# Global attention in a four-block transformer kernel: the row maxima are turned by a transposing transfer instead of TensorE, two steps earlier, and the output copy moves between two exponentials

## The reference, cut to what matters

```python
q = rope((x @ Wq).reshape(b, s, 32, 8)) * 8 ** -0.5      # 32 half-heads of 8 features
k = rope((x @ Wk).reshape(b, s, 32, 8))
v = (x @ Wv).reshape(b, s, 16, 16)
probs = softmax(q k^T)                                   # 1024 x 1024 for each half-head
w = probs[:, :, 0] - lam * probs[:, :, 1]                # pairs of half-heads
attn = w @ v; attn = attn * rsqrt(mean(attn ** 2) + eps) * subln_g * (1 - LAMBDA_INIT)
out = attn @ Wo
```

## Time and profile before

| | |
|---|---|
| median of 3 runs | 8230.22 us (8227.03 to 8234.33) |
| profiled execution, its own time | 8237.83 us |
| its span | 8234.0 us |
| PE, DVE, ACT, POOL busy | 92%, 84%, 76%, 45% |
| PE clock granted, mean | 0.958 of full |
| DVE reduces L1468 | 4096, busy 4678.2 us |
| ACT exponentials L1558 | 8192, busy 4389.4 us |

### The profile page before, as it was taken

How to read it: one execution, slowest core, us unless ns; L and a number is a source line. 1 busy time by engine, 2 the same in 40 slices (tenths; PEclk the granted TensorE clock), 3 DMA queues, 4 the chain that set the end, 5 groups by cost and what they waited for, 6 DMA issues and landing times. The chain is left out here.

```text
span 8234.0 us, 165474 instructions
## 1 busy us (share of the span) xinstructions
PE 7547.1 (92%) x64704; PEld 2707.9 (33%) x64704; DVE 6911.5 (84%) x8963; ACT 6265.2 (76%) x11486; POOL 3687.1 (45%) x5442
## 2 busy tenths in 40 slices
PE   6999988999889998899988999889998999989999
PEld 4322343223432234322343223432234322343223
DVE  5899768997689976899768997699966999669996
ACT  3599756997569975699756997569975699756996
POOL 3366333662336623366234662346613466134661
PEclk9899989999999998999999999999999999989999
DMA  0111001110011100111001110011100111001110
GB/s 31 46 39 36 25 12 49 36 40 20 12 51 36 39 19 12 51 39 36 19 12 52 39 35 20 9 54 38 39 19 7 57 35 39 21 3 58 37 38 23
DMA packets 462888, 264.15 MB, mean 32 GB/s; under 512 B 351798, under 2 KB 387126, under 8 KB 462070
## 3 DMA queue, kind: packets, MB, share of 16 engines
q1 hardware_dynamic: 462076, 253.24, 11.9%
HBM read 123.83 MB, written 67.37 MB: 23 GB/s over the span
## 5 line engine op out<-in xcount | busy, mean ns | idle before, releaser
L1468 DVE TENSOR_REDUCE mfull<-ps 128x1 f32<-128x1024 f32 x4096 | 4678.2, 1217 | 131.9 <-PE ps L1397 130.3
L1558 ACT ACTIVATE work<-ps 128x512 f32<-128x512 f32 x8192 | 4389.4, 596 | 287.1 <-PE ps L1418 164.0
L1432 PE MATMUL ps<-work,vbuf 128*32 128x256 f32 x32768 | 2624.1, 392 | 118.7 <-ACT hh L1570 118.7
L1397 PE MATMUL ps<-kop,qop 48*128 48x512 bf16 x8192 | 2505.2, 387 | 45.4 <-DVE mfull L1468 24.4
L1418 PE MATMUL ps<-qop,kop 51*128 51x512 bf16 x8192 | 2496.0, 385 | 2.3 <-DMA qop<-mT 2.3
L1432 PEld LDWEIGHTS ps<-work,vbuf 128*32 128x32 f32 x32768 | 654.4, 108 | 1720.4 <-ACT work L1558 865.3
L1418 PEld LDWEIGHTS ps<-qop,kop 51*128 51x128 bf16 x8192 | 495.2, 93 | 1734.4 <-ACT work L1558 1578.5
L254 POOL TENSOR_TENSOR rstd<-rstd,nhalf 128x8 f32<-128x8 f32 x64 | 109.4, 1709 | 1655.3 <-DVE rstd L248 1655.3
L1494 POOL CAST mpart<-mfull 128x16 bf16<-128x16 f32 x256 | 50.6, 198 | 1629.2 <-DVE mfull L1468 1574.5
L446 POOL TENSOR_TENSOR hh<-work,hmask 128x1024 f32<-128x1024 f32 x256 | 516.8, 2047 | 457.8 <-POOLq L1669 335.4
L1524 POOL TENSOR_TENSOR work<-work,none 128x16 f32<-128x16 f32 x224 | 650.5, 2904 | 18.1
(11 more groups left out here) (186 smaller groups left out, 9046.6 us busy)
## 6 DMA issues: line engine op xcount, KB each, us to landing
qop<-scratch SPq DMA_DIRECT2D x512, 64.0 KB
scratch<-work SPq DMA_DIRECT2D x32, 768.0 KB, 4.1
scratch<-hh SPq DMA_DIRECT2D x32, 768.0 KB, 3.6
kop<-scratch SPq DMA_DIRECT2D x256, 96.0 KB
vbuf<-in_x SPq DMA_DIRECT2D x9, 2048.0 KB, 8.2
qop<-scratch SPq DMA_DIRECT2D x512, 32.0 KB
kop<-scratch SPq DMA_DIRECT2D x256, 64.0 KB
qop<-mT SPq DMA_DIRECT2D x1024, 3.0 KB
```

The source lines that it names most:

```text
L1397: pe.matmul(ps[:, b + n, :], qop[r:r + KQ, s, i, t * P:(t + 1) * P], kop[r:r + KQ, s, i, half(n)], start=True, stop=True).then_inc(s_ms, 1)
L1432: mm = pe.matmul(ps[VW * i:VW * (i + 1), OB, cols], vp[:, b, t, (G * gl + i) // 2, :], prob[:, u % PS, i, cols], start=t == 0 and part == ...
L1468: v.tensor_reduce(mfull[:, m // CUT % 2, r // ROWS * G // 2 + i, to:to + 1], ps[:, b:b + NB, :].rearrange("p b n -> p (b n)"), AX.X, ALU.m ...
L1558: act.activation(prob[:, u % PS, hl, :], ps[:, EB[slot % len(EB)], :], ACT.Exp, scale=scale).then_inc(s_ex, 1)
```

## The change

The transpose of the maxima leaves PE and ACT. `mpart` becomes 128 x 4 x 128 bf16 (24 of each 128 columns are written, the rest is set to zero once), and SP issues a transposing transfer of the whole 128 x 512 tile into `mT`, waits for its landing, and then places the rows in `qop` with two transfers instead of four. `turn_maxima`, `keep_maxima`, the identity in bf16 and the slot in the rotation of the banks are gone. AHEAD goes from 23 to 25, so all maximum work and `cut` stand two steps earlier on the clock against the exponentials. On ACT, `keep_output` stands between the two exponentials of its step instead of behind them. PE's, POOL's and SP's other orders stay.

```diff
-        mpart = sb("mpart", [P, G, PARTS, T // 2], BF16)
-        mT = sb("mT", [PARTS * G * T // 2, P], BF16)
+        mpart = sb("mpart", [P, T // 2, P], BF16)
+        mT = sb("mT", [P, T // 2, P], BF16)
...
+                pool.memset(mpart[:, :, :], 0.0).then_inc(s_c, 1)
...
-            AHEAD = CUT + 7
+            AHEAD = CUT + 9
...
-            MAXIMA = [CUT * (h + 1) - 1 + TURN - AHEAD for h in range(NB * GROUPS)]
+            PLACED = [CUT * (h + 1) - 1 + TURN - AHEAD for h in range(NB * GROUPS)]
...
                     def maxima(h):
                         g, n = h // NB, h % NB
                         s = g % SLOTS
-                        sp.wait_ge(s_ex, maxima_slot(h) + 1)
+                        sp.wait_ge(s_mc, CUTS * (h + 1))
+                        if h >= 1:
+                            sp.wait_ge(s_md[(h - 1) // NB % SLOTS], placed(h - 1))
+                        sp.dma_start(mT[:, :, :], mpart[:, :, :].rearrange("p t c -> p (t c)"), transpose=True).then_inc(s_tm, 16)
+                        sp.wait_ge(s_tm, 16 * (h + 1))
                         for side in range(2):
-                            for i in range(G // 2):
-                                r0, k = ROWS * side + KQ, PARTS * T // 2 * (side * G // 2 + i)
-                                sp.dma_start(qop[r0:r0 + PARTS, s, i, half(n)].rearrange("s (t n) -> s t n", n=P),
-                                             mT[k:k + PARTS * T // 2, :]).then_inc(s_md[s], 16)
+                            r0, k = ROWS * side + KQ, PARTS * G // 2 * side
+                            sp.dma_start(qop[r0:r0 + PARTS, s, :, half(n)],
+                                         mT[k:k + PARTS * G // 2, :, :].rearrange("c t n -> c (t n)")).then_inc(s_md[s], 16)
...
-                    def turn_maxima(h):
-                        pe.wait_ge(s_mc, CUTS * (h + 1))
-                        bank_for(maxima_slot(h))
-                        pe.transpose(turn_at(h), mpart[:, :, :, :].rearrange("p h s t -> p (h s t)"),
-                                     identb[:, :]).then_inc(s_sc, 1)
...
-                        if e in MAXIMA:
-                            turn_maxima(MAXIMA.index(e))
...
                         if h >= 1:
-                            pool.wait_ge(s_sc, maxima_slot(h - 1) + 1)
-                        link(pool.tensor_copy(mpart[:, :, 0, :], mfull[:, s]))
+                            pool.wait_ge(s_tm, 16 * h)
+                        link(pool.tensor_copy(cutparts[:, :, 0], by_side(mfull[:, s])))
...
-                    def keep_maxima(h):
-                        act.wait_ge(s_sc, maxima_slot(h) + 1)
-                        if h >= 1:
-                            act.wait_ge(s_md[(h - 1) // NB % SLOTS], placed(h - 1))
-                        act.copy(mT[:, :], turn_at(h)).then_inc(s_ex, 1)
...
                     for e in CLOCK:
-                        if 0 <= e < LAST:
-                            for n in range(NB):
+                        due = tile_due(e, 1)
+                        for n in range(NB):
+                            if 0 <= e < LAST:
                                 exponentials(NB * e + n)
-                        if e in MAXIMA:
-                            keep_maxima(MAXIMA.index(e))
-                        if tile_due(e, 1) is not None and tile_due(e, 1) % T == T - 1:
-                            keep_output(tile_due(e, 1))
+                            if n == 0 and due is not None and due % T == T - 1:
+                                keep_output(due)
```

More of the change, by code:

```diff
@@ L206, in _ @@
             def _(act):
-                act.wait_ge(s_v0, 16)
+                act.wait_ge(s_v0, 15)
                 act.activation(lt[:, 2:4], lt[:, 0:2], ACT.Exp).then_inc(s_lam, 1)
@@ L230, in _ @@
                 pool.tensor_tensor(rstd[:, :], rstd[:, :], nhalf[:, :], ALU.pow).then_inc(s_c, 1)
-                pool.wait_ge(s_c, 4)
+                pool.wait_ge(s_c, 5)
             @block.sync
@@ L1267, in diff_attention @@
             s_mr = sem("da_mr")
-            s_mc = sem("da_mc")
+            s_mc, s_tm = sem("da_mc"), sem("da_tm")
             s_sc, s_ex, s_pv, s_oe = sem("da_sc"), sem("da_ex"), sem("da_pv"), sem("da_oe")
@@ L1297, in exp_tile @@
                 return u, u // (NB * T), u // T % NB, u % T, hl
[L1299 to L1305, removed]
             def max_bank(m):
@@ L1314, in value_tile, with by_side @@
                 return T + i // 2 if i % 2 == 1 and 0 <= i < 2 * T else None
-            def turn_at(h):
-                return ps[0:PARTS * CUT, EB[maxima_slot(h) % len(EB)], 0:P // 2].bitcast(BF16)
+            cutparts = mpart[:, :, 0:PARTS * G].rearrange("p t (a s i) -> p a s i t", a=2, s=PARTS)
+            def by_side(ap):
+                return ap.rearrange("p (a i) t -> p a i t", a=2)
             def placed(h):
-                return 64 * (h // NB // SLOTS * NB + h % NB + 1)
+                return 32 * (h // NB // SLOTS * NB + h % NB + 1)
             def at(e, after):
@@ L1384, in _ @@
                             turn(EARLY.index(e))
-                        if e in MAXIMA:
-                            maxima(MAXIMA.index(e))
+                        if e in PLACED:
+                            maxima(PLACED.index(e))
                 @block.tensor
@@ L1416, in exp_scores @@
                             pe.wait_ge(s_md[s], placed(k // STEPS))
-                        bank = bank_for(slot_of(k))
+                        bank = bank_for(k)
                         pe.matmul(ps[:, bank, :], kop[r:r + KM, s, i, t * P:(t + 1) * P],
@@ L1426, in values @@
                         if part == 0:
-                            pe.wait_ge(s_ex, slot_of(G * (u + 1) - 1) + 1)
+                            pe.wait_ge(s_ex, G * (u + 1))
                             if t == 0 and u >= 1:
@@ L1440, in _ @@
                             project_values(pe, value_tile(e))
-                        if e == MAXIMA[0]:
+                        if e == PLACED[0]:
                             pe.wait_ge(s_ve, TT // 2)
@@ L1492, in cut @@
                         if h >= 1:
-                            pool.wait_ge(s_sc, maxima_slot(h - 1) + 1)
-                        link(pool.tensor_copy(mpart[:, :, 0, :], mfull[:, s]))
-                        link(pool.tensor_tensor(mrem[:, 0], mfull[:, s], mpart[:, :, 0, :], ALU.subtract))
-                        link(pool.tensor_copy(mpart[:, :, 1, :], mrem[:, 0]))
-                        link(pool.tensor_tensor(mrem[:, 1], mrem[:, 0], mpart[:, :, 1, :], ALU.subtract))
-                        link(pool.tensor_copy(mpart[:, :, 2, :], mrem[:, 1]))
+                            pool.wait_ge(s_tm, 16 * h)
+                        link(pool.tensor_copy(cutparts[:, :, 0], by_side(mfull[:, s])))
+                        link(pool.tensor_tensor(by_side(mrem[:, 0]), by_side(mfull[:, s]), cutparts[:, :, 0], ALU.subtract))
+                        link(pool.tensor_copy(cutparts[:, :, 1], by_side(mrem[:, 0])))
+                        link(pool.tensor_tensor(by_side(mrem[:, 1]), by_side(mrem[:, 0]), cutparts[:, :, 1], ALU.subtract))
+                        link(pool.tensor_copy(cutparts[:, :, 2], by_side(mrem[:, 1])))
                     def planes(j):
@@ L1553, in exponentials @@
                         u, g, n, t, hl = exp_tile(k)
-                        slot = slot_of(k)
+                        slot = k
                         if u >= PS and k % G == 0:
```

7 lines of the change are left out of this document (2 added, 5 removed).

## The result

The changed kernel took 8181.33 us (8166.85 to 8185.19, 4 runs) against 8228.62 us before: ratio 0.9936, 95% interval 0.9924 to 0.9947, so 0.64% faster. In a second set of runs, experiment 5, it was 8161.81 us, ratio 0.9925 (0.9909 to 0.9942). The forecast was 8162 us, a ratio of 0.9918, with a range of 8138 to 8202. The profiled execution took 8183.91 us, with a span of 8179.8; before it was 8237.83.

A forecast was written before the change was run, and what follows sets the result against it. PE, with two long steps, bounds a half at 18.45 us, DVE's 18.16 just under. 10.9 us gained less 2.33 lost is 8.5 a pair, 68 over 8 pairs: 8230.22 - 68 = 8162 us, range 8138 to 8202.

The forecast's parts named there:

- PE bounds, with two long steps: Attention half before: PE's 14 ordinary steps of 1.105 us plus 1.32 and 1.66 make 18.45, DVE's 18.16 just under.
- the turn: Transpose of the maxima on PE: removing it gives back 0.21 us of each half in PE's chain.
- The copy's new place: Output copy between two exponentials: PE loses 0.34 plus 0.11, 0.45 us instead of 0.55 a half; ACT idles 0.27.
- The half after, 18.19 us: Half after both parts: PE 18.13, DVE 18.16, some stall reaching DVE; 0.35 us less than the mean of 18.54.
- Two more steps: Prologue of each pair: the first exponential comes 2.33 us later after the first reduce, added in full.
- The new chain, 5.2 us, hidden: Cut's end to placed maxima: transpose 2.5 us, placements and signals, 5.2 in sum, hidden with 2.8 us to spare.
- lies beside PE and is worth nothing by itself: Copy to `mT` on ACT, 0.25 us a half: its removal by itself was to gain nothing.
- They move with step 0: First exponential steps, at about half clock for 10 us: they shift with the start of the exponentials, nothing added.
- 31 x 0.35: Gain over the 31 turns and copies inside a pair's 512 exponential steps: 10.9 us.
- Rival 3, the late chain: Chain of the maxima takes 9.0 us, PE stands 1.0 us in each half: slower, 8410 us; chance 0.08.

The follow-up runs named there:

- experiment 5: The changed kernel measured once more, nothing altered: 8161.81 us, ratio 0.9925.
- experiment 3: The kernel before with only the output copy moved between the two exponentials; PE still turns the maxima, AHEAD 23: 8208.25 us, ratio 0.9975.
- experiment 2: The changed kernel with the output copy back behind both exponentials; transposing transfer and AHEAD 25 stay: 8192.13 us, ratio 0.9958.
- experiment 1: The changed kernel plus a small exponential on ACT behind the value projection's copies, so the table loads early: 8154.99 us, ratio 0.991.
- experiment 11: The changed kernel with the early table load and AHEAD 21 instead of 25, to make the chain late on purpose: 10740.48 us.
- experiment 7: The changed kernel with the early table load and AHEAD 23 instead of 25: 8151.4 us, ratio 0.9905.
- experiment 12: The changed kernel with the early table load and AHEAD 25, the kernel of experiment 1 measured again: 8153.51 us, ratio 0.9902.
- experiment 9: The changed kernel with early table load, AHEAD 24 and the maximum pass's half-heads reordered, so a step's two scores lie on different rows: 8152.43 us, ratio 0.9902.
- experiment 4: The changed kernel with AHEAD 23 instead of 25, nothing else: 8157.13 us, ratio 0.9914.
- experiment 8: The changed kernel with the early table load and AHEAD 22 instead of 25, which puts a step's two scores on the same rows: 14869.2 us.
- experiment 6: The changed kernel with the early table load and AHEAD 24 instead of 25, which puts both scores on the same rows: 14876.24 us, ratio 1.8075.
- experiment 10: The kernel of experiment 1, AHEAD 25, with the maximum pass's half-heads reordered so both scores of a step lie on the same rows: 14885.29 us.

## Why the prediction was right, and where not

- **PE bounds, with two long steps.** Right. Each taken away alone gave its own amount: the copy 0.10 us a half (experiment 3, forecast 0.10), the turn 18.49 to 18.27 = 0.22 (experiment 2, forecast 0.21 and a little behind it).
- **The copy's new place.** Right in both parts, 0.34 and 0.11 us of stall. ACT's idle time is 0.19 and not 0.27; why stays open, and it changed nothing.
- **The half after, 18.19 us.** 18.18 measured, and 18.20 in the mean of 30, which is the figure to set against the 18.54 of before: 0.34 a half, forecast 0.35. No gap of DVE is left that the timeline shows.
- **Two more steps: 2.33 us in full.** 2.34 in experiment 1.
- **The new chain, 5.2 us, hidden.** 5.1 us by its parts and 5.2 in experiment 11, and the row was the right price for the transpose: 2.4 us. The Trainium skill, "VectorE: DVE Perf Modes", section "The three transpose paths", gives 1309 ns for a transfer of 128 x 128; the forecast's estimate from it, 5.2 us for four tiles, was over twice what the trace shows. In 77 of 256 halves the transpose took over 3 us, up to 4.5; the forecast had priced only the longest case. 7.5 us were there, not 7.96, and the wait of `exp_scores` for the transfer is gone from the list of waits but for a single 0.4 us.
- **What failed is the sentence that the copy to `mT` "lies beside PE and is worth nothing by itself".** It was also what the table load waited behind, and without it the load falls behind the wait for the first score. The term is missing from the sum: 1.36 us to the first exponential in each pair, 8 x 1.36 = 11 us. With it the forecast would have been 57 us instead of 68; the eight pairs of the profiled executions gave 53, and the two measured medians lie 47 and 69 under those of before. The Trainium skill, "ScalarE: Activation LUTs", section "What ACT_TABLE_LOAD costs", gives 1283 ns for the load and a drain of some 1380 ns with it; the rows show the 1.28 us, and no drain behind it (7457.21 + 1.28 to 7458.51).
- **"They move with step 0" failed too.** The slow steps begin some 22 us after the first reduce in both kernels, though the first exponential moved from 26.3 to 30.0 us after it. To add nothing for them was right in size for the pair looked at, and within one kernel the clock makes up to 2.9 us of a pair.
- **Luck.** The 11.02 us behind the first exponential are not 31 x 0.35, near as they are. The 30 halves gave 30 x (18.54 - 18.20) = 10.2, the steps up to the first output copy 0.9 (24.38 to 23.48), and the last interval between copies took 0.1 back. That the median of experiment 5 lies on the forecast of 8162 is luck as well, since 22 us of its difference to the first set lie outside the attention.
- **The clock in the prologue.** It falls to 0.5 in some pairs and costs 7 us for each. The profiles have 1 such pair of 8 before and 2 of 8 in experiment 3, which turns on PE as well; 2 after; one in experiments 7 and 12, 4 in experiment 9, and none in experiments 1, 2, 4 and 5. Whether the change makes it more frequent can't be settled with one profile for each set of runs. Left open.
- **Rival 3, the late chain**, was not met, and not priced as such by any run: experiment 8 was covered by the rows, experiment 11 by POOL's order. Those two say that the schedule has hard edges close by, which the forecast did not price.

## What to carry to other kernels

When an instruction is taken out, look at what stands next behind it on its engine: a table load, or a wait, that it carried takes its place, and a load that was free can land on the chain that starts a stage. When two costs lie on a chain just above another engine's floor, price each against the chain and cut the sum at the floor; here that gave the half to 0.01 us. And a distance on a hand-made clock is no free number: check which pairs of matmuls share rows and which operations change places in an engine's list before it is moved by one.

## What the runs showed of the hardware that was not expected

- Two matmuls of 48 and 51 rows start together when they lie on different rows (3466.34 both at full clock, experiment 9; 4463.83 both at half clock, experiment 11), and one after the other on the same rows (6000.75 and 6001.15, experiment 6).
- In that serial form the granted clock stayed at 0.50, the level of 1.2 GHz, over a stretch of 1350 us with PE busy all through (experiments 6, 8 and 10), and at 1.00 in the paired form (experiment 9): 2.83 us a step against 1.14. "TensorE: Matmul & The Clock Gate" of the Trainium skill, Part 1, says that activity releases the throttle; here a PE that the profile shows as busy for the whole stretch stayed at the lower level, and why is not shown. What each part costs can be read at half clock alone: a step in pairs takes 1.98 us there (experiment 11), so that the serial form costs 0.85 us more and the lower clock 0.87 over the 1.105 of a paired step at full clock. No run shows the serial form at full clock.
- A transposing transfer of 128 x 512 16-bit elements landed in 2.39 to 2.44 us when no packet of instructions ran beside it (111 of them, kernel after), and in up to 4.5 us when one did.
- ACT_TABLE_LOAD waits for what the first exponential behind it waits for: it started at 7457.21 with the first score, after 10.89 us of idle time, and at 7420.59 once a small exponential stood ahead of it (experiment 1).
- A standstill of PE of 8.7 us was followed by 6 us at half clock (experiment 11), so that it costs more than its length.
